# Three reorderings in the first stage of a four-layer kernel: banks of W1's product, the next exponential, the routing weights

## The reference

```python
# block 1: linear attention and an MLP
q = x @ Wq
feat = elu(q) + 1                      # = exp(min(q, 0)) + max(q, 0)
KV, Ksum = feat^T q / L, sum(feat)     # per head, over one batch element
msg = (feat KV) / (feat Ksum + eps) * L
msg = msg @ Wm
y = x + LN(msg, g1, b1) + LN(relu(msg @ W1) @ W2, g2, b2)
x1 = LN(x + y)
# block 2: router over 64 experts, top 8 of each token
logits = x1 @ router_w.T
w = softmax(logits) kept at the 8 largest, divided by their sum
keys  = rank of each token within its expert (a cumulative sum), for the gather
# then: 64 routed experts and a shared one, block 3 (gated attention), block 4 (8 experts)
```

## Time and profile before

| | |
|---|---|
| timed runs | 648.25 us median of 3 (645.24 to 648.62) |
| profiled execution, its own time | 652.67 us |
| its span | 650.7 us |
| mean granted TensorE clock | 0.897 of full |
| busy, share of the span | PE 86%, DVE 71%, POOL 66%, ACT 47% |
| first stage | 0 to about 137 us |

### The profile page before, as it was taken

How to read it: one execution, slowest core, us unless ns; L and a number is a source line. 1 busy time by engine, 2 the same in 40 slices (tenths; PEclk the granted TensorE clock), 3 DMA queues, 4 the chain that set the end, 5 groups by cost and what they waited for, 6 DMA issues and landing times.

```text
span 650.7 us, 10440 instructions
## 1 busy us (share of the span) xinstructions
PE 562.6 (86%) x3231; PEld 459.8 (71%) x3231; DVE 462.1 (71%) x1568; ACT 305.8 (47%) x825; POOL 427.9 (66%) x471
## 2 busy tenths in 40 slices
PE   5889888899238877999899999999999999999993
PEld 4678777855226655787687887878878788788762
DVE  1577877789949423576677879778787787886873
ACT  3667756449201111225364736636456365463440
POOL 5453422319574576538887988979979799753673
PEclk9999989799555555579999999999999999999998
DMA  4688455789320121142330030300302100000000
GB/s 130 170 229 316 186 218 196 313 255 233 80 73 28 47 61 50 37 170 99 127 131 2 8 138 9 135 4 10 138 9 93 46 9 9 2 17 0 10 8 17
DMA packets 47225, 62.04 MB, mean 95 GB/s; under 512 B 13026, under 2 KB 39873, under 8 KB 46146
## 3 DMA queue, kind: packets, MB, share of 16 engines
q1 hardware_dynamic: 44610, 56.15, 26.8%
q0 software_dynamic: 2560, 5.23, 2.8%
HBM read 35.16 MB, written 24.13 MB: 91 GB/s over the span
## 4 chain that ended last, share of the span: by engine, by line
PE 59%; DVE 19%; issue 6%; ACT 6%; POOL 3%; DMA 3%; another core or an unknown queue 2%; SPq 1%; POOLq 0%; DVEq 0%; ACTq 0%
PE pair L1446 8%; PE pair L1448 8%; PE pair L1447 8%; PE pair L1779 5%; DVE c_g L1247 2%; PE pair L602 2%; PE pair L628 2%; PE pair L1558 2%; DVE cand L1975 2%; PE pair L1494 2%; PE pair L1789 2%; PE pair L1568 2%; PE pair L555 2%; POOL c_acc L959 2%
## 5 line engine op out<-in xcount | busy, mean ns | idle before, releaser
L959 POOL TENSOR_TENSOR c_acc<-c_acc,c_g 128x512 f32<-128x512 f32 x112 | 144.6, 1291 | 37.6 <-DVE c_g L1247 30.0
L1095 ACT ACTIVATE c_sg<-pair 128x256 f32<-128x256 f32 x256 | 95.3, 385 | 93.3 <-PE pair L1448 90.4
L1247 DVE SCALAR_TENSOR_TENSOR c_g<-pair,c_comb,c_sg 128x256 f32<-128x256 f32 x224 | 100.4, 478 | 27.0 <-ACT c_sg L1095 22.7
L1446 PE MATMUL pair<-c_w_hi,c_x3h 128*128 128x512 f32 x256 | 108.9, 426 | 12.2 <-DVE c_g L1247 11.3
L1448 PE MATMUL pair<-c_w_hi,c_x3l 128*128 128x512 f32 x256 | 101.0, 395 | 0.0
L1447 PE MATMUL pair<-c_w_lo,c_x3h 128*128 128x512 f32 x256 | 100.7, 393 | 0.0
L1446 PEld LDWEIGHTS pair<-c_w_hi,c_x3h 128*128 128x128 f32 x256 | 48.2, 188 | 23.5 <-DVE c_g L1247 14.2
L1448 PEld LDWEIGHTS pair<-c_w_hi,c_x3l 128*128 128x128 f32 x256 | 48.0, 188 | 11.2
L1447 PEld LDWEIGHTS pair<-c_w_lo,c_x3h 128*128 128x128 f32 x256 | 48.3, 189 | 8.0
L1857 POOL DMA_INDIRECT routed_rows<-x1T_all,dest_row x32 | 31.7, 992 | 28.9 <-DVE x1T_all L1769 21.2
L1852 POOL DMA_INDIRECT rows_all<-token_rows,tok_row x32 | 31.3, 978 | 14.8 <-issue 9.4
(11 more groups left out here) (374 smaller groups left out, 1489.3 us busy)
## 6 DMA issues: line engine op xcount, KB each, us to landing
routed_rows<-rows_all SPq DMA_DIRECT2D x8, 2048.0 KB
c_c<-routed_rows SPq DMA_DIRECT2D x7, 2048.0 KB, 7.8
token_rows<-a_xw SPq DMA_DIRECT2D x8, 384.0 KB, 2.8
a_x<-in_L_attn_x SPq DMA_DIRECT2D x8, 256.0 KB, 3.0
base_all<-a_xw SPq DMA_DIRECT2D x8, 256.0 KB, 3.5
c_c<-routed_rows SPq DMA_DIRECT2D x4, 512.0 KB, 5.2
out<-c_outb SPq DMA_DIRECT2D x16, 128.0 KB, 1.8
wgu_late<-in_L_ffn_w_gate SPq DMA_DIRECT2D x4, 480.0 KB, 7.7
```

The source lines that it names most:

```text
L959: g.tensor_tensor(acc, acc, b["g"][:, (2 * uf + i) % 4, :, :], ALU.add).then_inc(s["acc"], 1)
L1095: a_.activation(b[f"sg{q % 2}"][:, x, :], self.pair[q % 2][:, x, H1:2 * H1], SIG).then_inc(s["sig"], 1)
L1247: v.scalar_tensor_tensor(out=dst, in0=self.pair[q % 2][:, x, 0:H1], scalar=b[f"comb{uf}"][:, j * E1 + e:j * E1 + e + 1], in1=b[f"sg{q % 2} ...
L1446: t.matmul(dst, w_hi, x_hi, start=start, stop=False)
```

## The change

Four edits in `StageA`:

1. W1's product writes its first half to bank 6 and its second to bank 5, and waits for the logits' copy only ahead of the second half. ACT's two ReLU copies read the banks in that order.
2. Where the next block is ahead, its exponential is issued on ACT before the message's copy instead of after it.
3. On DVE the sum, the reciprocal and the routing weights of block k-3 are issued before the message of block k instead of after it.
4. `unread` issues four matmuls in place of six (twenty stay for the last block).

```diff
                 act.wait_ge(s["hT_mm"], 2 * n + 1)
                 if n:
                     act.wait_ge(s["l_mm"], n)
-                a.activation(b["hT"][:, 0, :], bank[5][:, :], ACT.Relu).then_inc(s["hT_sb"], 1)
+                a.activation(b["hT"][:, 0, :], bank[6][:, :], ACT.Relu).then_inc(s["hT_sb"], 1)
                 act.wait_ge(s["hT_mm"], 2 * n + 2)
-                a.activation(b["hT"][:, 1, :], bank[6][:, :], ACT.Relu).then_inc(s["hT_sb"], 1)
+                a.activation(b["hT"][:, 1, :], bank[5][:, :], ACT.Relu).then_inc(s["hT_sb"], 1)
...
             if k + 1 < self.N and not self.ahead(k + 1):
                 copy_xT(k + 1)
+            if self.ahead(k + 1):
+                exponential(k + 1)
             n = k
             if n < self.N:
                 act.wait_ge(s["msgT_mm"], n + 1)
...
             if k + 1 < self.N:
                 if not self.ahead(k + 1):
                     read_q(k + 1)
-                exponential(k + 1)
+                    exponential(k + 1)
...
                 v.tensor_tensor(by_half(ex), by_half(ex), mask, ALU.mult).then_inc(s["pick"], 1)
+            if 0 <= m < self.N:
+                dve.wait_ge(s["pick"], 5 * m + 3)
+                v.tensor_reduce(b["esum"][:, :], ex, AX.X, ALU.add).then_inc(s["pick"], 1)
+                dve.wait_ge(s["pick"], 5 * m + 4)
+                v.reciprocal(b["esum"][:, :], b["esum"][:, :]).then_inc(s["pick"], 1)
+                dve.wait_ge(s["pick"], 5 * m + 5)
+                if m >= 2:
+                    dve.wait_ge(self.xw_stored[m % 2], 32 * (m // 2))
+                v.tensor_tensor(b[f"xw{m % 2}"][:, :, D:ROW], ex, bcast_last(b["esum"][:, :], E0), ALU.mult).then_inc(s["w_sb"], 1)
             n = k
             if n < self.N:
                 num = pair[3][:, :, 0:2 * (D + H0)].rearrange("p b (t c) -> p b t c", c=D + H0)
...
                 ins.then_inc(s["msg_sb"], 1)
-            if 0 <= m < self.N:
...
-                v.tensor_tensor(b[f"xw{m % 2}"][:, :, D:ROW], ex, bcast_last(b["esum"][:, :], E0), ALU.mult).then_inc(s["w_sb"], 1)
...
-                if n >= 2:
-                    pe.wait_ge(s["lg_sb"], n - 1)
                 for h in range(2):
-                    t.matmul(bank[5 + h][:, :], b["WmW1"][:, h * D:(h + 1) * D], b["msgT"][:, :], start=True, stop=True).then_inc(s["hT_mm"], 1)
+                    if h and n >= 2:
+                        pe.wait_ge(s["lg_sb"], n - 1)
+                    t.matmul(bank[6 - h][:, :], b["WmW1"][:, h * D:(h + 1) * D], b["msgT"][:, :], start=True, stop=True).then_inc(s["hT_mm"], 1)
...
-                unread(20 if n == self.N - 1 else 6, bank[0])
+                unread(20 if n == self.N - 1 else 4, bank[0])
```

## The result

The changed kernel takes 641.37 us, the median of 9 executions (638.5 to 645.27), against 648.62 us (645.24 to 651.45) for the kernel before, measured beside it. The ratio on record is 0.9879, 95% interval 0.9852 to 0.9906: 7.8 us less, between 6.1 and 9.6. It is an estimate from all the executions and not the quotient of the medians, which lie 7.25 us apart. The forecast was 642.8 us, in a range from 640.2 to 646.2.

A forecast was written before the change was run, and what follows sets the result against it. No engine is full; a chain changing engine bounds the first stage's rounds, with L602 waiting for the logits' copy. Terms sum to 5.09 us: 648.25 - 5.09 - 0.4 (clock) = 642.8 us, range 640.2 to 646.2.

The forecast's parts named there:

- The start: In k=0 the earlier exponential delays the message's copy: a loss of 0.28 us, bound 0.6 for two rounds.
- The plain rounds: k=3 to 6: L602's first half no longer waits for the logits' copy; 0.82 us each, 3.28 us over four.
- The key write of k=6: With the routing weights moved ahead, L547 starts directly behind L667: 0.46 us, bounds 0 and 0.51.
- k=7 and k=8: Late rounds: L602's first half is done during the wait for the logits' copy, saving 0.98 and 0.65 us.
- The sum: Whole first stage: 3.28 + 0.46 + 0.98 + 0.65 - 0.28 = 5.09 us saved.
- The clock: From L577's end to L602, 3.33 us becomes about 2.95; fewer falls credited with 0.4 us, bounds 0 and 1.63.
- the fall of the clock goes too: Rival, chance 0.18: the median before contains a fall that the shorter stretch to L602 removes, 1.63 us; 641.5 us.
- the forecast by itself: The forecast case for the whole kernel, chance 0.51: 642.8 us, by itself 641.8 to 644.2.
- DVE was no bound: Answers a rival, chance 0.15: DVE's order holds back each plain round by half, losing 1.64 us; 644.8 us.
- the change doesn't do what it says: Rival, chance 0.11: L602's second half waits as before or the message's copy is late; 2.8 us saved, 645.4 us.
- The slower one, by the clock: Rival, chance 0.05: fewer unread products, so the clock falls ahead of all six starts k=3 to 8; 651.6 us.

The follow-up runs named there:

- the hole filled: Kernel before plus three unread products behind L685 in k=2 to 5, where L602 waits for the logits' copy: 631.9 us against 633.66, ratio 0.9975.

## Why the prediction was right

**The start.** Forecast a loss of 0.28 us. Measured 0.99 - 0.73 = 0.26 us. In k=1 the delay was absorbed by the wait for feat, as argued: the wait is 0.48 us, was 0.74. The way on was another than the one I named. TensorE waited for x in the first trace of before alone; in the changed kernel no trace shows that wait, and yet it is 24.71 us from L299 of k=0 to L604 of k=3, against 24.46 without the earlier exponential. TensorE's own order carries the delay on.

**The plain rounds.** Forecast 0.82 us each, measured 12.89 - 11.97 = 0.92: 3.7 us over four in place of 3.28. The mechanism was right and the term a little small: L604 starts 0.84 us behind the start of L687 (I took 0.89, which is 0.05), and the products cut bring 0.06 us, which I had put at nothing with a bound of 0.1. A reading beside it was further off: I left DVE 1.5 us idle in a round, and it has 0.75. Its busy time rose from 10.56 to 11.22 us, for the most part by the adds of the next paragraph.

**The key write of k=6.** Forecast 0.46 us, measured 0.42 by the weights alone. The form of 1.4 us is gone:

```profile
L502 DVE TENSOR_TENSOR a_xw<-a_ex,a_esum x8: 424/424/426, 50.1 to 127.3; 128x256 f32<-128x256 f32 x8
```

The largest of eight is 426 ns, was 1407. The price has moved to the adds of the plain rounds. They start earlier now against POOL's L262 and lie beside nearly all of it; the first two lines are of the kernel before, where they lay beside a part of it:

```profile
66.35 1.28 POOL L262 TENSOR_TENSOR a_r<-a_x,a_b 128x512 f32<-128x512 f32 x1
67.01 1.55 DVE L530 SCALAR_TENSOR_TENSOR a_r<-a_gm,a_rstd,a_r 128x128 f32<-128x128 f32 x4
...
64.73 1.26 POOL L262 TENSOR_TENSOR a_r<-a_x,a_b 128x512 f32<-128x512 f32 x1
64.80 2.13 DVE L532 SCALAR_TENSOR_TENSOR a_r<-a_gm,a_rstd,a_r 128x128 f32<-128x128 f32 x4 [0.33 <-POOL a_rstd L254]
67.04 1.14 DVE L532 SCALAR_TENSOR_TENSOR a_r<-a_gl,a_rstd,a_r 128x128 f32<-128x128 f32 x4
```

Four adds of this form take 1.14 us without POOL and 2.13 beside it, 0.99 us more, where L262 has 1.19 us to go when they start; before, with 0.62 us of L262 left, it was 1.55. With the routing weights alone moved they also take 2.13 us in plain rounds. The three lengths grow with the time beside L262; why is not shown. So in plain rounds the move gave DVE nothing. The prediction had assumed no gain there, but without this reason, and feat still came in time.

**k=7 and k=8.** Forecast 0.98 and 0.65 us. From the key write to the first L606/L608 it is 101.30 - 95.45 = 5.85 us before and 94.84 - 89.90 = 4.94 after: 0.91. From there to L602/L604 of k=8 it is 10.49 and 9.77 us: 0.72.

**The sum.** 3.7 + 0.4 + 0.9 + 0.7 - 0.26 = 5.4 us, in place of the 5.09 forecast. A direct reading agrees: from L299 of k=0 to the third key write it is 133.77 - 19.03 = 114.74 us with the hole filled and 127.69 - 18.44 = 109.25 after the change, 5.5 less, and neither trace has a fall in its plain rounds.

**The clock.** This is the term that was mis-sized: 0.4 us, one in four of one fall. The 1.63 us in it are what L602 of k=6 takes more than at the other three plain starts of that trace, 1.95 to 1.96 us each, at a granted clock of 1.00 and with the same wait of 0.72 us ahead. The stretch from the last unread product to L604 got shorter as expected, 67.08 - 64.26 = 2.82 us for 3.33 (I had 2.95). The kernel before with its hole filled shows 1.6 us (0.4 to 2.8 by its interval), which I put down to the clock alone: about one fall of 1.69 us in each execution on average. 5.4 + 1.6 = 7.0 us, against 7.8 (6.1 to 9.6) measured, and 7.25 between the medians. That the changed kernel has no falls left is what its traces show; the executions without a trace leave it open. What I called a rival, "the fall of the clock goes too", with 641.5 us, is what came, at 641.37; that it is so close is luck, since the measurement leaves more than 1 us either way. The step of the prediction that failed is the reading of one fall in four starts as a low chance. Counted by execution and not by start, one fall in four starts is one fall in that execution. How many there are on average is known from the filled kernel's time only, 0.4 to 2.8 us at 1.69, so 0.2 to 1.7 falls; of the two traces of before one has a fall. The time lies 0.4 us below the band given for the forecast by itself, 641.8 to 644.2, less than the measurement resolves. The two profiled executions exaggerate the gain: 650.7 - 639.7 = 11.0 us of span, since the trace of before holds a fall that cost 1.69 us in k=6 and its L606 and, at the stage's end, a longer L685 (1.97 us in k=8, 1.24 after) and unread products that held up the transposes behind them until 1.46 us after the end of L350 (0.05 after). At the third key write the two traces are 136.26 - 127.69 = 8.6 us apart.

**The other rivals.** DVE was no bound, though it has 0.75 us of idle time left in a round and L508 starts without a wait. That the change doesn't do what it says is refuted by L604's missing wait. The times given for these two rivals leave out the 0.4 us that the forecast takes for the clock; with it they would be 0.4 lower. The slower one, by the clock, has runs behind it: four products alone cost 1.5 to 2.9 us, with a fall in one round of the trace, and none at all brings falls in four rounds. It didn't come about here; the exchange of banks closes more of the stretch than the cut opens (3.70 us with four products alone, 2.82 in the changed kernel), which fits, though one trace of each doesn't prove it.

## What to carry to other kernels

When one instruction of a pair waits for a buffer, let the half that needs another buffer go first: of the four edits this one made most of the gain (5.7 of 7.8 us by the ratios), and where the wait was real (k=7) it still brought 0.91 us, near the first half's length of 0.98. A filler such as these unread products is to be judged together with the hole behind it: cutting it from six to four cost 1.5 to 2.9 us with the hole open, and with the hole closed no trace with four had a fall in its plain rounds. So cut it after the hole is closed, not before. And a fall of the clock seen once among n equal rounds must be counted per execution, with a trace or two more, before its price is put into a sum.

## What the runs showed of the hardware

Work that nobody reads, put into a wait of TensorE, made the kernel before faster by 1.6 us (0.4 to 2.8), and the changed kernel without any took 5.2 us more than with six products a round. Four float32 adds on DVE took 1.14 us alone, 1.55 beside a part of POOL's L262 and 2.13 beside nearly all of it. The fall comes and goes between executions of one kernel (one in k=6 in the first trace of before, none in the second). The chips differ by more than the change: the kernel before took 633.66 us on one and 649.17 and 649.74 on the other occasions. In the traces the first stage is alike there (third key write at 127.68 us in the changed kernel with six products on the fast chip, 127.69 in the changed kernel's first trace). From there to the first product of block 3, L1448 at 268.77 and at 284.41 us, it is 141.1 and 156.7 us: the difference arises in the search and the expert phase, not in what was changed. Why was not tried.
